# First attention of a two-layer transformer kernel: stack-ordered scratch, small operations behind value products, eight heads in one bank, three first-score banks

## The reference, cut to what matters

```
qkv = einsum('bsd,ed->bse', x, w_qkv);  q, k, v = split(qkv, 3)     # 16 heads of 8
q, k = rope(q), rope(k)
attn = softmax(q @ k.T / sqrt(8))                                   # per head, 256 x 256
out  = einsum('bsd,ed->bse', attn @ v, w_out) + b_out
x    = layernorm(x + out)
```

## Time and profile before

| | us |
|---|---|
| median of three runs | 1610.42 (1604.62 to 1614.15) |
| profiled execution, its own time | 1616.59 |
| its span, first to last instruction | 1614.8 |
| TensorE, VectorE, ScalarE, GpSimd busy | 1532.2, 1241.5, 1071.4, 926.6 |
| first exponential of first attention starts | 52.4 |
| first exponential of second attention starts | 758.7 |
| mean granted TensorE clock | 0.964 |

### The profile page before, as it was taken

One profiled execution on the slowest core, in us unless ns is written; L12 is line 12 of the kernel. 1 busy time (PEld: TensorE's weight loads), 2 busy tenths in 40 slices (PEclk: granted clock), 3 DMA queues, 4 the chain that ended last, 5 costly groups with the idle time before them and its releaser, 6 DMA issues. The chain is left out here.

```text
span 1614.8 us, 56003 instructions
## 1 busy us (share of the span) xinstructions
PE 1532.2 (95%) x17772; PEld 1149.4 (71%) x17772; DVE 1241.5 (77%) x3420; ACT 1071.4 (66%) x2596; POOL 926.6 (57%) x1065
## 2 busy tenths in 40 slices
PE   5999999999999899996999999999999999998998
PEld 3444444444444368884888888898888888897997
DVE  6778788888878648885788887888887878874666
ACT  0577777777767667873767777777777777774332
POOL 4444445444534126656687777887777887772222
PEclk7899999999989889996999999999999999999999
DMA  7333333333333200003222222222222222210211
GB/s 205 108 100 112 99 110 99 113 95 117 100 101 98 63 21 29 29 30 103 69 76 79 81 66 85 77 79 76 77 72 85 74 81 76 69 44 21 66 62 52
DMA packets 170169, 129.08 MB, mean 80 GB/s; under 512 B 13036, under 2 KB 143224, under 8 KB 170104
## 3 DMA queue, kind: packets, MB, share of 16 engines
q1 hardware_dynamic: 169136, 127.65, 25.7%
q10 hardware_dynamic: 968, 0.60, 0.1%
HBM read 60.56 MB, written 54.53 MB: 71 GB/s over the span
## 5 line engine op out<-in xcount | busy, mean ns | idle before, releaser
L867 DVE TENSOR_REDUCE shifts<-bank 128x2 bf16<-128x512 f32 x1024 | 689.1, 690 | 182.2 <-PE bank L1017 176.9
L815 ACT ACTIVATE probs<-bank 128x512 f32<-128x512 f32 x1024 | 576.9, 593 | 132.4 <-PE bank L1003 124.8
L965 PE MATMUL bank<-values,probs 64*128 64x129 f32 x8192 | 580.0, 277 | 3.9 <-DVE o_even L835 0.7
L965 PEld LDWEIGHTS bank<-values,probs 64*128 64x128 f32 x8192 | 527.2, 188 | 31.0 <-issue 10.9
L1003 PE MATMUL bank<-q_stack,k_stack 49*128 49x256 bf16 x2048 | 388.7, 277 | 28.8 <-DMA q_stack<-shift_rows 24.8
L1017 PE MATMUL bank<-k_stack,q_stack 48*128 48x256 bf16 x2048 | 384.7, 279 | 8.7 <-DVE shifts L867 5.6
L622 POOL TENSOR_TENSOR values<-mix,v_in 128x1024 f32<-128x1024 f32 x128 | 302.3, 2363 | 0.0
L1003 PEld LDWEIGHTS bank<-q_stack,k_stack 49*128 49x128 bf16 x2048 | 158.7, 95 | 158.5 <-issue 70.5
L631 POOL TENSOR_TENSOR o_odd<-o_odd,scaled 128x256 f32<-128x256 f32 x224 | 163.6, 731 | 161.6 <-ACT scaled L738 161.5
L738 ACT ACTIVATE scaled<-bank,recips 128x128 f32<-128x128 f32 x448 | 138.0, 358 | 88.2 <-DVE recips L861 88.2
L955 PE MATMUL bank<-probs,values 128*32 128x256 f32 x2048 | 170.8, 407 | 0.0
(11 more groups left out here) (169 smaller groups left out, 2187.2 us busy)
## 6 DMA issues: line engine op xcount, KB each, us to landing
score_parts<-parts SPq DMA_DIRECT2D x128, 192.0 KB, 2.3
k_stack<-score_parts SPq DMA_DIRECT2D x256, 96.0 KB
q_stack<-score_parts SPq DMA_DIRECT2D x256, 96.0 KB
score_parts<-parts SPq DMA_DIRECT2D x128, 128.0 KB, 2.3
score_parts<-parts SPq DMA_DIRECT2D x128, 64.0 KB, 1.8
x_in_f<-x_all SPq DMA_DIRECT2D x64, 128.0 KB, 2.0
x_in<-in_L_attn_x SPq DMA_DIRECT2D x32, 128.0 KB, 3.1
q_stack<-shift_rows SPq DMA_DIRECT2D x256, 2.0 KB
```

Source lines behind the costliest of these rows:

```text
L815: act.activation(probs[:, s % RING, :, :].rearrange("p t n -> p (t n)"), s2[s % 2][:, :], ACT.Exp, scale=scale).then_inc(exp_done, 1)
L867: dve.tensor_reduce(shifts[:, :, hf, col], s1[s % 2][:, :].rearrange("p (t n) -> p t n", t=TILES), op=ALU.max, axis=AX.X, negate=True).the ...
L965: return pe.matmul(pv_bank(h)[:, q * (D + 1):(q + 1) * (D + 1)], probs[rows, h % RING, t, q * P:(q + 1) * P], values[b.odd][rows, t, h, :] ...
```

## The change

In first attention:

- Slots: V moves from 14 to 10, the transpose of x from 0 (three batches ahead) to 14 (four ahead), K from 5 to 6, heads from 8 and 6 to 7 alone, the output projection from 13 to 15. Every small operation now follows a slot with products. ScalarE's copies of o, shifts and x come one or two slots after TensorE's operation.
- Banks: first scores get a third bank (`s1_order`), in exchange for the second bank of products. The products of eight heads go into one bank: each head's 32 columns of values are taken from a place 16 columns further left for every second group, so that its 9 rows land beside those of the other group. Two copies and four transposes take the place of four and eight.
- The scratch tensor has the order of the stack (64 rows for each parity, of which 16 are filled once with ones at the start), so that one transfer reads both sides and both parities. The parts are written in ten transfers. `parts` is double. One transfer writes the rows of shifts of both parities.
- GpSimd copies x for V; ScalarE normalises; the statistics come a step later.

`prepare` sets both stacks to ones and writes the 16 free rows to the scratch, at the head of SyncE's queue. Second attention gets the double `parts` and the single transfer of shift rows. The loop of `attn0` begins at step 4.

```
         self.shifts1 = 2 if first else 1
         self.shifts0 = 11 if first else 9
-        self.v, self.v_ahead = (14, 1) if first else (13, 2)
-        self.xt = 0 if first else 13
+        self.v, self.v_ahead = (10, 1) if first else (13, 2)
+        self.xt, self.xt_ahead = (14, 4) if first else (13, 3)
         self.q, self.q_ahead = (3, 3) if first else (1, 2)
-        self.k = 5 if first else None
-        self.heads = (8, 6) if first else ()
+        self.k = 6 if first else None
+        self.heads = 7 if first else None
         self.ot = 11 if first else 9
-        self.out = 13 if first else 11
-        self.norm, self.norm_lag = (2, 2) if first else (15, 1)
+        self.out = 15 if first else 11
+        self.norm, self.norm_lag = (5, 2) if first else (15, 1)
+        self.factor_lag = 2 if first else 1
...
+        sp.wait_ge(stacks_set, 3)
+        for side in range(2):
+            for parity in range(2):
+                sp.dma_start(scratch[side, parity, USED:SLOTS, :, :].rearrange("s (d r) n -> (s d) (r n)", r=PAIRS),
+                             core.stack[0][0:(SLOTS - USED) * HD, side, :, :].rearrange("p r n -> p (r n)")
+                             ).then_inc(free_slots_written, 16)
...
-        for stack in core.k_stack:
-            pool.memset(stack[:, :, :], 1.0).then_inc(stacks_set, 1)
+        for stack in core.stack:
+            pool.memset(stack[:, :, :, :].rearrange("p e r n -> p (e r n)"), 1.0).then_inc(stacks_set, 1)
...
-    s1, s2 = b[0:2], b[2:4]
-    pv, m0, m1 = (b[4:6], b[6], b[7]) if first else (b[4:7], b[7], b[7])
+    s1, s2 = (b[0:3], b[3:5]) if first else (b[0:2], b[2:4])
+    pv, m0, m1 = (b[5:6], b[6], b[7]) if first else (b[4:7], b[7], b[7])
+    s1_order = (0, 1, 2) * 4 + (0, 1) * 2 if first else (0, 1) * 8
...
+        def parts_out_in_stack_order(b):
             for parity in range(2):
+                split = parts[b.odd][parity * TILE_ROWS:(parity + 1) * TILE_ROWS, :, :, :]
+                for s, m in RUNS[:2]:
+                    q = K_PART[s]
+                    to = scratch[:, parity, s:s + m, :, :].rearrange("e s r n -> e r s n")
+                    sp.dma_start(to[0], split[:, 0:m, 1, :]).then_inc(parts_written, 16)
+                    sp.dma_start(to[1], split[:, q:q + 1, 0, :].broadcast_to([TILE_ROWS, m, TOK])).then_inc(parts_written, 16)
+                k_and_q = split.rearrange("p k e n -> p (k e) n")[:, 1:5:3, :]
+                sp.dma_start(scratch[:, parity, USED - 1, :, :].rearrange("e r n -> r e n"), k_and_q).then_inc(parts_written, 16)
...
+            if first:
+                src = scratch.rearrange("e a s (d r) n -> e (a s d) r n", r=PAIRS)[:, :, prs, :]
+                sp.dma_start(core.stack[b.odd][:, :, prs, :].rearrange("p e r n -> p e (r n)"),
+                             src.rearrange("e p r n -> p e (r n)")).then_inc(stacked[hf], 16)
+                return
...
+        def keep_x_for_v(i):
+            b = i.plus(2)
+            pool.wait_ge(xt_ready, times(i, 2, n))
+            wait(pool, v_in_psum, times(i, 0, n))
+            pool.tensor_tensor(x_v[b.odd][:, :], x_t[b.odd][:, :], core.zeros[:, :], op=ALU.add).then_inc(x_v_ready, 1)
...
+                start = h * VW - sub * (VW // 2)
+                last = pe.matmul(pv[0][VW * a:VW * (a + 1), 0:TOK],
+                                 values[b.odd][:, t, :, :].rearrange("p h c -> p (h c)")[:, start:start + VW],
+                                 probs[:, h % RING, t, :], start=(sub == 0 and t == 0), stop=(sub == 1 and t == TILES - 1),
                                  skip_group_check=True)
...
-                wait(pe, max_done, b.number() * HEADS + (s - 1))
+                wait(pe, max_done, s1_free(b, s))
```

More of the change, by code:

```diff
@@ L442, in attention @@
     b = [core.bank[k] for k in banks]
-    s1, s2 = b[0:2], b[2:4]
-    pv, m0, m1 = (b[4:6], b[6], b[7]) if first else (b[4:7], b[7], b[7])
+    s1, s2 = (b[0:3], b[3:5]) if first else (b[0:2], b[2:4])
+    pv, m0, m1 = (b[5:6], b[6], b[7]) if first else (b[4:7], b[7], b[7])
+    s1_order = (0, 1, 2) * 4 + (0, 1) * 2 if first else (0, 1) * 8
     groups = HEADS // 4
+    regions = groups // 2
     slots = Slots(first)
+    writes = 10 if first else 2 * len(RUNS)
+    reads = 1 if first else 4
     def sb(name, shape, dt=FP32):
@@ L458, in attention @@
     rest = sb("rest", [P, sides, TOK])
-    parts = sb("parts", [P, 3, sides, TOK], BF16)
+    parts = [sb(f"parts{k}", [P, 3, sides, TOK], BF16) for k in range(2)]
     shifts = sb("shifts", [P, TILES, 2, half_heads if first else P], BF16)
@@ L771, in step @@
                 if s == 3 and first and on(-1):
-                    take_heads(i.plus(-1), 3)
-                if first and s == slots.v and on(1):
+                    take_heads(i.plus(-1), 1)
+                if first and s in (slots.norm, slots.norm + 1) and on(-2):
+                    norm(i.plus(-2), (s - slots.norm,))
+                if first and s == slots.v + 1 and on(1):
                     b = i.plus(1)
@@ L871, in step @@
             for s in range(HEADS):
-                if s in slots.heads and on(-1):
-                    recip_heads(i, slots.heads.index(s))
+                if s == slots.heads and on(-1):
+                    recip_heads(i)
                 if not first and on(0 if s >= 4 else -1):
@@ L880, in step @@
                     max_of_head(i.plus(1), s)
-                if s in slots.heads and on(-1):
-                    scale_heads(i, slots.heads.index(s))
+                if s == slots.heads and on(-1):
+                    for sub in range(2):
+                        scale_heads(i, sub)
                 if first and s in (slots.q, slots.k) and on(3):
@@ L939, in shifts_turned @@
                 to = SHIFTS_AT + t * P
-                last = pe.transpose(m0[:, :].bitcast(BF16)[0:half_heads if first else P, to:to + P], shifts[:, t, hf, :],
+                last = pe.transpose((m1, m0)[hf][:, :].bitcast(BF16)[0:half_heads if first else P, to:to + P], shifts[:, t, hf, :],
                                     core.ident_bf[:, :])
@@ L1095, in others_of_first @@
                 wait(pe, o_ready, times(i, -1, n) * 2)
+                wait(pe, qk_taken, times(i, 3, n) * 2 - 1)
+                shifts_turned(i.plus(1), 0)
+            if s == slots.xt and on(slots.xt_ahead):
+                b = i.plus(slots.xt_ahead)
+                pe.wait_ge(x_loaded[b.odd], (b.half + 1) * 16)
+                wait(pe, v_taken, times(i, 1, n))
                 wait(pe, qk_taken, times(i, 3, n) * 2)
-                wait(pe, shift_rows_ready, times(i, 0, n) * 2)
-                shifts_turned(i.plus(1), 0)
+                for t in range(TILES):
+                    last = pe.transpose(m0[:, t * P:(t + 1) * P], x_in[b.odd][:, t, :], core.ident[:, :])
+                last.then_inc(xt_in_psum, 1)
             if s == slots.out and on(-1):
                 pe.wait_ge(ot_ready, times(i, -1, n))
+                if on(1):
+                    pe.wait_ge(shift_rows_ready, i.plus(1).number() * 2 + 1)
                 for t in range(TILES):
@@ L1727, in build @@
         places[0].close()
-        attn1 = attention(nc, core, 1, (2, 3, 5, 6, 7, 1, 4, 0), scratch, places[3], before=ffn0_)
+        attn1 = attention(nc, core, 1, (2, 3, 5, 6, 7, 1, 4, 0), by_slot, places[3], before=ffn0_)
         places[2].close()
```

284 lines of the change are left out of this document (140 added, 144 removed).

## The result

The changed kernel took 1638.46 us (median of 4 runs, 1636.73 to 1639.96) beside 1607.52 us for the kernel before (4 runs, 1598.64 to 1614.15): ratio 1.0187, 95% interval 1.0147 to 1.0227. A second comparison of the two later gave 1638.98 beside 1614.83, ratio 1.0144 [1.0115, 1.0173]. The forecast was 1632 in 1600 to 1660, slower at 0.81. So the sign and the size came out. That the size did is partly luck: the start was forecast 9 us too low, the steps 5 us too high, the rest of the kernel 3 us too high, and these errors cancel. The medians themselves differ by 31 us in the first comparison and by 24 in the second, beside a forecast of 22 (the profiled execution took 1639.96, forecast 1639; the 6 us taken off for the median are 1.5): the kernel before varies by 10 to 24 us within a comparison, the changed one by 3 to 6.

The account below looks back on a forecast made before the run. TensorE's in-order queue was taken to set first attention's step. Steps +15 and start +7 made +22 us, the profiled 1616.6 becoming 1639; with the median 6 us lower, forecast 1632, range 1600 to 1660.

Parts of the forecast that it names:

- The pairs: First attention: two neighbouring slots without products take at least 1.15 us (0.43 + 0.60 + 0.12), waiting for the exponential.
- Operations behind products: First attention, per step: TensorE's small operations cost their full price after products, K 1.06, 5.03 us in all.
- The step after: First attention's step in the changed kernel: 7.12 + 4.60 + 5.03 = 16.75 us, plus 0.15 for small waits, taken as 16.9.
- The difference over the steps: First attention: a step of 16.9 against 16.43 us, +0.47, over 31 steps +15 us.
- The start: Preparation up to the first scores: longer memsets delay the loads of x, +8, the first step gives one back: +7 us.
- The third bank, 0.: First scores in first attention: the added bank lets TensorE run ahead of VectorE, which already keeps up: 0 us.
- VectorE, ScalarE, GpSimd: First attention: the changed work of these engines does not bind the step, costed at 0 us.
- The shift row: First attention's step boundary: TensorE's wait of 0.7 us a step goes, with a free queue and one transfer.
- Rival (a): First attention: pairs not held by the exponential, or operations run under products; 15.0 us a step, 1574 us; chance 0.12.
- Rival (b): First attention: many short TensorE waits make the granted clock fall, one fall every other step, +26, 1658 us; chance 0.12.
- Rival (c): First attention: the DMA loop through the scratch comes 0.8 us late each step, +25, 1657 us; chance 0.10.
- Rival (d): Whole kernel: no change, unseen waits of 0.5 us a step vanish and the start is hidden, 1607 to 1615; chance 0.06.

Follow-up runs that it names:

- half maxima: The changed kernel with first attention's maximum taken over 128 of the 256 keys: 1634.78 us (one run).
- the kernel with both repairs of the start: The changed kernel with the third batch's x loaded ahead of the large loads, free rows written behind them, memsets of k_stack alone: 1625.07 us, ratio 1.0064.

## Why the prediction was right, and where it was not

*The pairs* (forecast at least 1.15). Right in mechanism: four waits a step, all for ScalarE, and the exponential is a term of the pair one for one. The size is 1.08 = 0.43 + 0.60 + 0.05, by which the lower end that the prediction gave, 1.15, was 0.07 too high. In the earlier trace rows the pair had the heads' transposes under it, whose own time could set 304.93 as well, so the 0.12 behind the exponential was an upper end.

*Operations behind products* (5.03 in all). Right: K itself takes 1.07 there (forecast 1.06) and its slot grows by 1.14; V, o with shifts, x and the output come out within 0.08 of their prices.

*The step after*, 16.75 + 0.15. Measured 16.86: pairs 4 x 0.07 less, slot 1 0.13 more (1.12, where 0.89 + 0.10 make 0.99, which half maxima give), and slots 5, 9 and 13, each behind a pair, 0.08 more each (the late first scores in the loop): -0.28 + 0.13 + 0.24 = +0.09, and 16.84.

*The difference over the steps*, forecast +15, measured +9.6. This comes from both ends of a small difference. The kernel before took 512.3 / 31 = 16.53 a step where the count of maxima gave 16.43 (a window's count is off by a few at its edges; 3 of 487 are this 0.10), which is 3 us; after took 16.84 where 16.9 was taken, which is 2.

*The start*, forecast +7, measured +16.5 at the first exponential. This is the step that failed. The chain from the memsets came out; the term left out is the third batch's transposes. The change takes x four batches ahead, so one more pair of transposes stands ahead of the weights' preparation in TensorE's order, and its load stands behind x_all in the queue. The prediction costed the moved transposes on TensorE and not what they wait for. Loading that x earlier gives 10.8 back at the first exponential, freeing the queue from the memsets 7.9, both with half the memsets 15.0.

*The third bank, 0.* Wrong as a price, though not in the sum, which went by the pairs and the start: without the bank the kernel is some 11 us slower. Of these 5 are the first scores of slots 5, 9 and 13 (31 x 0.17), held by the maximum of two slots before, and 2 are the later first second scores; the other 4 are not taken apart (two traces of one kernel differ by 2.4 in the first six steps alone). The prediction read VectorE's mean load in the steady stretch; it did not ask, slot by slot, whether a maximum or an exponential ends last. At the start VectorE is on the path besides (half maxima bring the first exponential 6.1 us forward).

*VectorE, ScalarE, GpSimd*, forecast 0: VectorE costs 0.13 a step in slot 1, through the bank of slot 15. ScalarE's copies cost nothing: all four pairs have the same 1.08.

*The shift row.* The wait went, as forecast, with the clock's falls. Of the two reasons given, a free queue holds and one transfer does not: alone it leaves 22.0 us. Nor does the queue need the new scratch to be free in time.

*Rival (a)*: no; the operations are not hidden and the pairs are held. Its sign, pairs under 1.1 us, did come (1.08): it was set too near to 1.15, and the waits for ScalarE and the pace of 16.86 decide. *Rival (b)*: the granted clock did not fall once from 72.4 to 570.8 us, with four waits of 0.47 us a step; before it had fallen 8 times from 100 to 545, for 3.4 us mostly, each time during or up to 2.1 us after a wait of 1.26 to 2.72 us for the shift row, as at 346.8 behind the wait of 1.26 at 344.78. The Trainium skill, page "TensorE: Matmul & The Clock Gate", section "A second HAM failure mode: psum-queue depth-cycling", tells of another kernel, with bfloat16 matmuls of 512 columns, in which frequent short idle times between groups made the clock swing. These 30 steps do not do so: short idle times between groups did not make the clock swing here. *Rival (c)*: the loop closes; first scores waited 0.5 us for the stacks in 460 us (L1068 above). *Rival (d)*: no.

## What to carry to other kernels

Where two banks go from TensorE through an activation and back, two neighbouring slots without products have a floor (here 1.08 us: 0.43 to the activation, 0.60 for it, 0.05 back), and independent operations belong under it: ordering them behind longer slots makes them pay twice. When an order is made to look further ahead, follow the first pass through it, and the queue position of each load that now comes first. A mean load does not say which wait ends last at one slot: a third bank whose engine had idle time was still worth 0.06 us in each slot behind a pair, and more at the start.

## What the runs showed of the hardware, unexpected

- Beside GpSimd's long memsets VectorE's small operations ended late: the cast of 128x128 that began at 1.52 took 7.21 us and the copy at 4.83 took 3.90, both ending at 8.73, with the memsets (8.64). In the kernel before, with two memsets of half the size, the same cast took 2.05 and ended at 3.57, behind the first of them (3.49), and copies from 4.81 on took 0.29 beside the second. In the kernel with both repairs of the start, with memsets of that same size, the cast took 3.79 and ended at 5.32, behind both (5.24). So it is not every operation beside a memset that is held. What waits for the weights' copies starts sooner in both (x's transposes at 6.32 and 6.83). That a memset holds the other engine's operations is how the ends read; it wasn't tried by itself.
- A memset of 4096 bf16 elements in 128 partitions takes 3.5 us (6.96 for two), twice that of 2048 (3.63 for two).
- The granted clock stayed at 1.00, which is 2.4 GHz, for 498 us with four gaps of 0.47 us in each 16.85; the kernel before, with hardly any of these gaps but with waits of up to 2.7 us at some step boundaries, had the falls.
- In a hardware loop, after a wait for ScalarE, the first scores started 0.08 us behind the second ones; in written-out steps of the same kernel both started at once (0.003).
- One read of 512 KB took 0.37 us to issue (four in its place 0.68 to 0.73 each) and landed 3.9 us later; the ten writes from 64 partitions took 0.61 each to issue, the six from 128 partitions 0.44 to 0.53.
